# Graph network: score maxima from TensorE's masked sums and plain maxima, and the stages around them reordered

## The reference

```python
Q = relu(x @ query_kernel + query_bias)[row]        # row, col: edges and self loops
K = relu(x @ key_kernel + key_bias)[col]
V = (x @ kernel)[col]
att = sum(Qh * Kh, axis=-1)                         # per edge and head
smax = segment_max(att, row)                        # per node and head
sexp = exp(att - smax[row])
alpha = sexp / segment_sum(sexp, row)[row]
out = segment_sum(Vh * alpha, row) + bias
```

## Time and profile before

| | us |
|---|---|
| three runs, device time | 2522.43, 2524.81, 2525.97 |
| median | 2524.81 |
| profiled execution, its own time | 2524.51 |
| its span | 2522.7 |

### The profile page before, as it was taken

How to read it: one execution, slowest core, us unless ns; L and a number is a source line. 1 busy time by engine, 2 the same in 40 slices (tenths; PEclk the granted TensorE clock), 3 DMA queues, 4 the chain that set the end, 5 groups by cost and what they waited for, 6 DMA issues and landing times. The chain is left out here.

```text
span 2522.7 us, 38976 instructions
## 1 busy us (share of the span) xinstructions
PE 2167.6 (86%) x12483; PEld 921.4 (37%) x12570; DVE 1981.2 (79%) x2690; ACT 1186.5 (47%) x1579; POOL 89.3 (4%) x147
## 2 busy tenths in 40 slices
PE   5888988899688888888888689898988889699998
PEld 3555555466332222222222222222222222255555
DVE  7887878333399999999999699898999989743223
ACT  4676766466511112111210587787877879300000
POOL 1000000110000000000000000000000000211000
PEclk9998999999799999999999899999999999899999
DMA  0000000266700000000000444344444434200000
GB/s 20 0 0 0 0 0 0 76 207 228 227 21 6 6 6 9 6 6 6 9 6 3 108 122 108 105 122 112 119 113 114 115 103 125 56 1 1 1 9 18
DMA packets 266004, 144.83 MB, mean 57 GB/s; under 512 B 169469, under 2 KB 260883, under 8 KB 265900
## 3 DMA queue, kind: packets, MB, share of 16 engines
q1 hardware_dynamic: 265094, 143.04, 20.3%
q10 hardware_dynamic: 806, 0.40, 0.1%
HBM read 103.43 MB, written 39.97 MB: 57 GB/s over the span
## 5 line engine op out<-in xcount | busy, mean ns | idle before, releaser
L1297 DVE CUSTOM_DVE_ANT_0 ps<-ps,max_mask 128x1536 f32<-128x1536 f32 (+1 forms) x400 | 700.7, 1864 | 14.5 <-PE ps L1251 14.5
L1550 DVE SCALAR_TENSOR_TENSOR counts<-counts,att_a 128x1792 f32<-128x1792 f32 x263 | 518.3, 2029 | 38.9 <-ACT counts L1530 38.9
L1530 ACT ACTIVATE counts<-ps 128x896 f32<-128x896 f32 x526 | 454.2, 916 | 180.9 <-PE ps L1474 179.4
L1474 PE MATMUL ps<-att_q,att_k 99*128 99x448 bf16 x1400 | 339.5, 366 | 49.6 <-issue 24.2
L1284 ACT ACTIVATE max_mask<-counts 128x3136 uint8 x24 | 67.6, 2816 | 528.6 <-DVE max_mall L1305 528.6
L480 ACT ACTIVATE counts<-ps 128x899 f32 x261 | 247.2, 947 | 135.5 <-PE ps L430 121.9
L1483 PE MATMUL ps<-counts,att_v 128*32 128x448 f32 x2104 | 260.6, 568 | 36.5 <-DVE counts L1550 8.1
L1474 PEld LDWEIGHTS ps<-att_q,att_k 99*128 99x128 bf16 x1400 | 110.4, 99 | 382.3 <-issue 169.9
L1251 PE MATMUL ps<-counts,max_q 96*128 96x512 bf16 (+1 forms) x700 | 170.0, 360 | 74.2 <-DVE max_mx L1297 52.2
L426 PE MATMUL ps<-hot 128*128 128x192 bf16 (+1 forms) x474 | 201.7, 442 | 32.3 <-DVE hot L331 32.3
L615 PE MATMUL ps<-counts 128*128 128x512 bf16 (+1 forms) x1036 | 205.7, 358 | 20.6 <-DVE counts L683 19.9
(11 more groups left out here) (209 smaller groups left out, 2471.6 us busy)
## 6 DMA issues: line engine op xcount, KB each, us to landing
att_k<-keys SPq DMA_DIRECT2D x175, 198.0 KB
att_v<-values SPq DMA_DIRECT2D x175, 128.0 KB
counts_turned<-counts SPq DMA_DIRECT2D x25, 784.0 KB, 5.0
att_a<-counts_turned SPq DMA_DIRECT2D x175, 112.0 KB
max_q<-queries SPq DMA_DIRECT2D x25, 192.0 KB, 3.0
att_q<-queries SPq DMA_DIRECT2D x7, 519.8 KB
queries<-fl_cuts SPq DMA_DIRECT2D x24, 128.0 KB
keys<-fl_cuts SPq DMA_DIRECT2D x24, 128.0 KB
```

What stands on the lines that cost most here:

```text
L1297: v.tensor_tensor_reduce(out=flat[:, lo:hi], in0=flat[:, lo:hi], in1=mask[slot][:, lo:hi], scale=1.0, scalar=0.0, op0=ALU.mult, op1=ALU.ma ...
L1474: last = nc.tensor.matmul(m.bank[2 * (n % NS) + z][:, 0:CW], k[i][:, 2 * h + z, :], q[:, 2 * h + z, :], start=True, stop=True)
L1530: nc.scalar.activation(e[n % NE][:, :, :], m.ps[:, 2 * (n % NS):2 * (n % NS) + 2, 0:CW], ACT.Exp).then_inc(exped, 1)
L1550: v.scalar_tensor_tensor(w, w, 1.0, a[i % DG][:, :].unsqueeze(1).to_broadcast([P, 4, CW]), op0=ALU.min, op1=ALU.mult).then_inc(weighed, 1)
```

## The change

*Edge count.* The adds and the load of their base addresses move from VectorE to GpSimd. ScalarE loads its base addresses four at a time (LOADED = 4), four times a body. VectorE's loop is left with the one-hots.

*Score maxima.* PSUM is split into two halves of four banks, taken in turn by every maximum. Behind the three or four score matmuls, TensorE adds, into the same columns, the product of a diagonal matrix of -1e30 and a bfloat16 mask that is 1 where there is no edge. VectorE takes a plain maximum. The fillers are gone. Parts are now the outer loop and heads the inner one. ScalarE makes the masks per part, three deep, by two passes (a copy whose accumulator gives the degree, and 1 minus the count, cut at zero). The maximum over the two parts stands at the end of each block. The loops are unrolled.

*Negated maxima.* They move into `attend`, which begins its loads at once; the split and turned rows of chunk 0 go from SBUF straight into the query tile by three small DMAs of ScalarE, and all rows are stored in DRAM by SP behind the first loads. The maxima are cut at zero from below.

*Chunk boundaries.* The queries come by four DMAs, one for each pair of heads. GpSimd adds the bias to the residual, adds that to the weighted rows, subtracts the mean and multiplies by the inverse root. VectorE's order becomes: weighting 0, sums, first half of weighting 1, division (`weigh_rows`), second half of 1, first half of 2, `statistics`, second half of 2. SP loads the second group of slots ahead of the store of the previous rows.

Cut to its core:

```diff
 count_edges
-                        while G * done + G - 1 <= T * q:
-                            add(BG * i + done, done % NSH, base[done - n0])
-                            done += 1
+        @block.gpsimd
+                def adds(i, n):
+                    base = nc.values_load_multi_w_load_instructions(
+                        t.gbase[0:1, ds(BG * i, n)], engines=(mybir.EngineType.Pool,), ...)[1]
+                    for k in range(n):
+                        pool.wait_ge(bank_free, BG * i + k + 1 + 4)
+                        pool.wait_ge(added, BG * i + k + NSH)
+                        column = m.counts[:, :, ds(base[k], 1)]
+                        pool.tensor_tensor(column, column, shared[k % NSH], op=ALU.add).then_inc(added, 1)
 scalar, evacuate
+                        if k % LOADED == 0:
+                            base = nc.values_load_multi_w_load_instructions(
+                                t.gbase[0:1, ds(BG * i + k, min(LOADED, n - k))], ...)[1]
 score_maxima, tensor
+                        if n >= 2:
+                            pe.wait_ge(maxed, n - 1)
+                        for col in range(lo, hi, 512):
+                            nc.tensor.matmul(halves[n % 2][:, col - lo:col - lo + w], q[b % 2][:, h, :],
+                                             kk[h][:, col:col + w], start=True, stop=False)
+                        if h == 0:
+                            pe.wait_ge(masked, NPT * b + part + 1)
+                        for col in range(lo, hi, 512):
+                            last = nc.tensor.matmul(halves[n % 2][:, col - lo:col - lo + w], far[:, :],
+                                                    mask[(NPT * b + part) % NM][:, col - lo:col - lo + w],
+                                                    start=False, stop=True)
 score_maxima, vector
-                        v.tensor_tensor_reduce(
-                            out=flat[:, lo:hi], in0=flat[:, lo:hi], in1=mask[slot][:, lo:hi],
-                            scale=1.0, scalar=0.0, op0=ALU.mult, op1=ALU.max,
-                            accum_out=mx[slot][:, h, part:part + 1]).then_inc(maxed, 1)
+                        v.tensor_reduce(mx[b % 2][:, h, part:part + 1], halves[n % 2][:, 0:hi - lo], axis=AX.X, op=ALU.max)\
+                         .then_inc(maxed, 1)
 attend, scalar
+            act.wait_ge(neg_copied, 1)
+            for z in range(3):
+                act.dma_start(q[KS + z:KS + z + 1, :, :], neg[z * HEADS:(z + 1) * HEADS, 0:CW]).then_inc(neg_placed, 16)
+                if n == NE - 2:
+                    act.wait_ge(neg_stored, 48)
+                    act.wait_ge(neg_placed, 48)
 attend, gpsimd
+                pool.tensor_tensor(xr[:, :, :], xr[:, :, :], bb[:, :].unsqueeze(1).to_broadcast([RB, RPC, D]),
+                                   op=ALU.add).then_inc(pool_step, 1)
+                pool.wait_ge(weighted, 2 * c + 2)
+                pool.tensor_tensor(y[:, :, :], y[:, :, :], xr[:, :, :], op=ALU.add).then_inc(mixed, 1)
                 inverse_roots(pool, m, mv, sd, normed, rooted, c)
+                pool.tensor_tensor(y[:, :, :], y[:, :, :], wide(mv[:, :, 0]), op=ALU.subtract).then_inc(pool_step, 1)
+                pool.tensor_tensor(y[:, :, :], y[:, :, :], wide(sd[:, :]), op=ALU.mult).then_inc(finished, 1)
 attend, vector
                 rest(c)
                 weights(c + 1, 0)
                 take_sums(c)
                 weights(c + 1, 1, range(1))
-                rows(c)
+                weigh_rows(c)
                 weights(c + 1, 1, range(1, 2))
+                weights(c + 1, 2, range(1))
+                statistics(c)
+                weights(c + 1, 2, range(1, 2))
```

More of the change, by code:

```diff
@@ L1366, in attend @@
-def attend(nc, m, x1, qs, ks, vd, ad, bias, out):
+        more = sb2("keys", [KS, HH // 2, NP], BF16)
+        kk = [m.spare[0:KS, h * NP:(h + 1) * NP] for h in range(HH // 2)] + [more[:, h, :] for h in range(HH // 2)]
+        q = [sb2(f"q{i}", [KS, HH, P], BF16) for i in range(2)]
+        NM = 3
+        NPT = len(PARTS)
+        PW = max(hi - lo for lo, hi in PARTS)
+        mask = [sb2(f"mask{i}", [P, PW], BF16) for i in range(NM)]
+        far = sb2("far", [P, P], BF16)
+        mx = [sb2(f"mx{i}", [P, HH, len(PARTS)], F32) for i in range(2)]
@@ new lines, in _, with make @@
+        @block.scalar
+        def _(act):
+            def make(b, part):
+                r = NPT * b + part
+                lo, hi = PARTS[part]
+                if r >= NM:
+                    act.wait_ge(scored, HH * (r - NM + 1))
+                nc.scalar.activation(mask[r % NM][:, 0:hi - lo], m.at[:, b, lo:hi], ACT.Copy,
+                                     accum_out=degree[part][:, b:b + 1]).then_inc(counted, 1)
+                act.wait_ge(counted, r + 1)
+                nc.scalar.activation(mask[r % NM][:, 0:hi - lo], m.at[:, b, lo:hi], ACT.Relu, bias=one[:, :], scale=-1.0)\
+                    .then_inc(masked, 1)
+            act.wait_ge(far_ready, 2)
+            for b in range(SB):
+                for part in range(NPT):
+                    make(b, part)
@@ new lines, in _ @@
+        @block.vector
+        def _(v):
+            v.tensor_single_scalar(far[:, :], m.identb[:, :], FAR, op=ALU.mult).then_inc(far_ready, 1)
+            v.memset(one[:, :], 1.0).then_inc(far_ready, 1)
+            for b in range(SB):
+                for part, (lo, hi) in enumerate(PARTS):
+                    for h in range(HH):
+                        n = per * b + HH * part + h
+                        v.wait_ge(scored, n + 1)
+                        v.tensor_reduce(mx[b % 2][:, h, part:part + 1], halves[n % 2][:, 0:hi - lo], axis=AX.X, op=ALU.max)\
+                         .then_inc(maxed, 1)
+                v.wait_ge(maxed, per * (b + 1))
+                v.tensor_reduce(mall[:, b, :], mx[b % 2][:, :, :], axis=AX.X, op=ALU.max)
+            v.wait_ge(counted, NPT * SB)
+            v.tensor_tensor(m.out_norm[:, :], degree[0][:, :], degree[1][:, :], op=ALU.add)
@@ L1424, in load_others @@
                     load_slot(c, 0, i)
+                for i in range(DG):
+                    load_slot(c, 1, i)
                 if c:
@@ L1516, in chunk @@
                             sums(c, d, d < 2, d >= 2 * SB - 2)
+            pe.wait_ge(neg_step, 5)
+            for b in range(SB):
+                last = nc.tensor.matmul(m.bank[b // 4][0:3 * HEADS, (b % 4) * P:(b % 4 + 1) * P],
+                                        pcs[:, b, :, :], m.identb[:, :], start=True, stop=True)
+                if b in (3, SB - 1):
+                    last.then_inc(neg_turned, 1)
+            pe.wait_ge(neg_copied, 3)
+            pe.wait_ge(neg_placed, 48)
             for c in range(NC):
@@ L1553, in rest @@
             def rest(c):
[L1555 removed]
+                for i in range(3, SB):
                     weights(c, i)
```

351 lines of the change are left out of this document (129 added, 222 removed).

## The result

The changed kernel takes 2456.94 us (median of 2453.34, 2455.77, 2458.12 and 2459.95) against 2524.13 (four runs): a ratio of 0.9733, 95% interval 0.9716 to 0.975, 67 us less. The forecast was 2471, its own range 2456 to 2488, so the time lies at the lower end of that range. The profiled execution took 2458.12 us with a span of 2456.4, 66.3 us less than the span before.

The account below looks back on a forecast made before the run. VectorE was taken to bound the maxima and attention, and its register loads to stall TensorE in the edge count. From 2524.5 us, -36 - 3 - 12 - 3 + 1 = -53 gave 2471 us, range 2456 to 2488.

Parts of the forecast that it names:

- Edge count: Edge-count stage: moving 16 register loads and 261 adds off VectorE ends TensorE's stall at each loop body, -36 us.
- Rival 1: Edge count: GpSimd's load and adds, or ScalarE's four loads, end last in each body; 2507 us, chance 0.09.
- Maxima: Score-maxima stage: plain maximum at 1.72 against 1.745 us each, -10, less two costs; together -3 us, bounds -19 to +23.
- rival 3: Maxima stage: the longer score path sets the period at 1.785 us, +26, 2497 us; chance 0.12.
- The two costs set against it: Maxima stage: dependent small reduction ending each of 25 blocks, +5 us; only one maximum ahead of the key wait, +2.
- To the first score: From the maxima to the attention's first score: query loads and placing of the maxima's rows run side by side, -12 us.
- Chunk boundaries: Six attention chunk boundaries: 3.1 - 3.9 - 1.0 + 1.3 = -0.5 us each, -3 us for six.
- stretched weightings: Chunk boundaries: GpSimd's passes hold the port 0.9 us each; three and the reciprocal root fall on busy weightings, +3.1 us.
- the wait added: Chunk boundaries: VectorE meets a later wait for the next scores and exponentials, about +1.3 us each.
- rival 2: Edge count and chunk boundaries: port held for the whole GpSimd instruction, +16 and +22 us, 2509 us; chance 0.10.
- Rival 4: Maxima stage: TensorE's clock falls to its lower level, 2.4 us per maximum, +260, 2731 us; chance 0.05.
- Rival 5: Maxima and chunk boundaries: the maxima reach 1.68 us and the port is held half as long, 2443 us; chance 0.08.

Follow-up runs that it names:

- the later block maximum: The changed kernel with the small maximum over the two parts taken one head into the next block, as before the change: 2453.18 us, ratio 0.9724.
- the two-load run: The changed kernel with a chunk's queries loaded by two DMAs (heads 0 and 1, then 2 to 7) instead of four: 2463.29 us, ratio 0.9758.

## Why the prediction was right

The stalls that it named are gone, and the edge count and the way to the first score came as worked out. The maxima and the chunk boundaries gained more than forecast, and at the boundaries one term came near its price by luck (below).

**Edge count** (-36 forecast, -34.6 measured). The step held: the 16 loads were the stall and TensorE is the bound. The prediction moved "the 16 register loads and 261 adds"; the gain belongs to the loads alone, and to their size: in fours they are covered by the rounds in stock. GpSimd's add of 29 elements takes 0.47 us on average (the group below: busy us, mean ns), above the 0.43 that was named as its upper end (the shortest took 0.32). Nobody waited for it. Rival 1 (another engine ends the body last) didn't come: GpSimd's load is 1.06 us, near the lower bound.

```profile
L397 POOL TENSOR_TENSOR counts<-counts,hot 128x29 bf16 x261 | 123.5, 473 | 291.0 <-ACT hot L481 290.8
```

**Maxima** (-3 forecast, -12.9 measured). This is the term that was mis-sized. The durations 1.75 and 1.82 were right, and VectorE does set the period. The prediction had only one dependent and one custom form to tell how far reductions overlap, and took 0.07 us; it is 0.085. So VectorE's own spacing was taken as 1.68 and 1.75, 1.715 on average, and measured 1.664 and 1.731, 1.70 on average. That is 7 of the 10 us. Another 2 come from the step to 1.72, taken because TensorE's path came out level, and 1.4 from 1.745 for the period before, which is 1.749 on average: 400 x 0.051 = -20 us, not -10. Level paths don't add up here: each maximum costs the later of the two. The path's estimate of 0.1 us from TensorE's end to VectorE's start was too long by some 0.05 (948.81 to 948.86), which is what rival 3's 1.785 rested on. The two costs set against it were right: 0.2 us for each block's end, of which the later block maximum wins back 3.3 us, and 2 to 3 us at the start.

**To the first score** (-12, -11.8). Placed rows and loads run side by side, as worked out. What ends last is the placing: TensorE's first score waits for `DMA att_q<-att_e`, the turned rows (they lie in the memory of `att_e`) on their way into the query tile. No run tests this part by itself; it is read from the two traces.

```profile
1353.08 5.07 PE L1407 MATMUL ps<-att_q,att_k 99*128 99x448 bf16 x14 [4.21 <-DMA att_q<-att_e]
```

**Chunk boundaries** (-0.5 each forecast, -1.5 measured). From the start of a chunk's last weighting to the start of the next chunk's 26th it took 62.86 us on average and takes 61.37. The terms: removed from VectorE -3.9 as forecast; the earlier queries -1.2 (forecast -1.0; the two-load run gives them back); stretched weightings +3.4 (forecast +3.1): of 23, 18 are 0.84 us longer and five, which meet the bias pass, 1.08. That leaves +0.2 or 0.3 for the later waits, where the prediction had +1.3: the waits of 0.45 and 0.53 us at the moved weightings are there, but smaller, and partly stand in place of older ones. So the step that failed in size is the wait added.

The stretch came near its price by luck. The prediction took a pass as 4 x 0.43 = 1.7 us, let VectorE lose half of it, and counted three passes and the inverse root. Where no weighting runs beside them (at the first and the last chunk) the additions last 1.26 us and the subtraction and the scaling 1.04; VectorE lost 0.84 us to each of three and 1.08 to the bias pass in five of six chunks, and nothing to the inverse root. The pass was shorter and the share lost larger.

**The port** (rival 2). At the boundaries the rival's mechanism came, with a shorter pass. The weighting issued at 1464.70 is as good as held until GpSimd's pass ends at 1465.67: 1464.70 + 2.86 - 2.02 = 1465.54. GpSimd is slower there too: its subtraction lasts 1.98 us at the boundary and 1.04 at the last chunk. The Trainium skill (SBUF — State Buffer, Who interferes with whom) says that VectorE with two SBUF inputs and GpSimd reading SBUF exclude each other for the whole instruction. The trace agrees here, with 0.84 us lost to passes of 1.04 to 1.26 us; where the rest of a pass lies isn't shown. The rival's +22 us didn't come because it took 1.7 us for a pass.

In the edge count the rival's sum used 0.43 us for an add of 29 elements beside every round and found a round too long by 0.08. The durations of a round's three one-hots add up to 1.80 us on average there, and to 1.72 before and with the adds on VectorE: 0.08 us more for a round, not 4/3 x 0.43 = 0.57. The rounds kept waiting for TensorE, so that price was hidden too.

**Rival 4** (the lower clock) didn't come: 0.98 in the maxima. It stayed there with one product fewer and was 0.50 without products. At that level four matmuls took 1.51 us, so eight would take an estimated 3.0, more than the period of 1.73.

**Rival 5** (better) came by half: the maxima reached 1.70 where it had 1.68, but a pass of GpSimd cost VectorE 0.84 us, near the 0.9 of the forecast and not half of it.

## What to carry to other kernels

Where an engine stalls its feeder once per loop body, look at what it does outside the busy rows (here a register load of 3.6 us), and split that before moving work away. Work given to GpSimd beside busy two-input instructions of VectorE on SBUF can still cost VectorE time (here 0.84 to 1.08 us for each wide pass): price it by the stretch it causes, and first look for waits of VectorE's own that could take it. Where two paths come out level, take the later one, then add a little work to the other, and take a little away, to see how much room it has; look at the granted clock of that run before reading it.

## What the runs showed of the hardware that was not expected

- A load of 16 registers took 3.6 us on VectorE, 1.06 on GpSimd and 1.02 on ScalarE; of four, 0.96 on VectorE and 0.31 on ScalarE.
- One wide pass of GpSimd that met back-to-back weightings (none of them stretched) shows 68.55 us in the trace where it takes 1.26 alone; GpSimd's spans are rough, but its end, 1669.37, is 1.1 us behind the end of that chunk's last weightings (1668.24), VectorE's first pause. So GpSimd was here the one that was kept out (GpSimd, then VectorE); what decides which of the two isn't shown:

```profile
1600.82 68.55 POOL L1389 TENSOR_TENSOR counts<-counts 112x512 f32<-112x512 f32 x1 [11.88 <-DMA counts<-state]
```

```profile
1664.28 3.96 DVE L1509 SCALAR_TENSOR_TENSOR counts<-counts,att_a 128x1792 f32<-128x1792 f32 x2
1669.76 2.03 DVE L1509 SCALAR_TENSOR_TENSOR counts<-counts,att_a 128x1792 f32<-128x1792 f32 x1 [1.52 <-ACT counts L1480]
```

- TensorE's granted clock in the maxima was 0.98 with twelve to sixteen matmuls for two maxima and with ten to fourteen, and 0.50 with six to eight. Without the products the time stayed (2455.25 us) all the same, since half the matmuls at the lower level last as long as all of them at the higher. Whether the kernel before needed its fillers for its 0.99 wasn't run.
